# Expert stage of a fused audio tower: another order of its rows, a shorter bias product, and the fold ahead of the weight transposes

## What is computed

```
tok:   a = x W1 + b1;  8 times: up = relu(a + shift_r(up) W2 + b2), down likewise;  h = relu(c + ...)
attn:  h = h + (exp(-gamma * |q - k|^2) v) Wo^T          8 heads of 64, no softmax
ffn:   x = layernorm(h);  logits = x gate_w + gate_b;  top 2 of 16 experts, softmax over the two
       moe = sum over the two of weight * (relu(x w1[e] + b1[e]) w2[e] + b2[e])
       h = h + layernorm(x + moe) * gamma + beta
```

## Time and profile before

| | |
|---|---|
| median of three runs | 789.38 us (787.16, 789.38, 789.58) |
| profiled execution | 787.81 us, span of its instructions 785.9 us |
| busy, share of span | PE 95%, weight loads (PEld) 55%, DVE 80%, ACT 68%, POOL 59% |
| granted PE clock, mean | 0.991 |
| expert stage | about 505 to 783 us, steps of 16.5 us |

### The profile page before, as it was taken

One profiled execution on the slowest core, in us unless ns is written; L12 is line 12 of the kernel. 1 busy time (PEld: TensorE's weight loads), 2 busy tenths in 40 slices (PEclk: granted clock), 3 DMA queues, 4 the chain that ended last, 5 costly groups with the idle time before them and its releaser, 6 DMA issues.

```text
span 785.9 us, 16799 instructions
## 1 busy us (share of the span) xinstructions
PE 746.5 (95%) x5712; PEld 430.0 (55%) x5712; DVE 626.9 (80%) x1525; ACT 533.9 (68%) x1058; POOL 460.9 (59%) x625
## 2 busy tenths in 40 slices
PE   2999999999999999999999998999999999999992
PEld 1444356666666666676666665444555555454440
DVE  7676778888888888878888785788888888888862
ACT  1566779888888888888898887644555555546442
POOL 7644324544546454564545532267788787887877
PEclk9999999999999999999999999999999999999997
DMA  6300202211221112211122112000000000000000
GB/s 182 97 2 2 55 1 55 46 36 30 54 55 36 36 39 54 55 29 40 43 55 55 27 38 46 1 2 1 9 15 9 8 8 8 11 13 7 9 7 20
DMA packets 22619, 25.46 MB, mean 32 GB/s; under 512 B 12520, under 2 KB 21480, under 8 KB 22408
## 3 DMA queue, kind: packets, MB, share of 16 engines
q1 hardware_dynamic: 21544, 23.14, 12.6%
q10 hardware_dynamic: 992, 1.26, 0.7%
HBM read 5.06 MB, written 2.43 MB: 10 GB/s over the span
## 4 chain that ended last, share of the span: by engine, by line
PE 72%; DVE 13%; issue 6%; ACT 6%; POOL 2%; DMA 1%; ACTq 1%; POOLq 0%; SPq 0%; DVEq 0%
PE bank L1325 14%; PE bank L1303 14%; PE bank L1204 10%; PE bank L1162 9%; PE bank L1228 6%; PE bank L1075 5%; DVE m L819 5%; DVE prob L865 4%; PE bank L1230 4%; PE bank L1065 2%; ACT prob L601 1%; ACT m1o L560 1%; ACT m1e L560 1%; PE bank L1350 1%; PE bank L1342 1%
## 5 line engine op out<-in xcount | busy, mean ns | idle before, releaser
L429 POOL TENSOR_TENSOR sq<-sq 125x256 f32<-125x256 f32 x128 | 97.4, 772 | 162.3 <-ACT sq L565 137.7
L865 DVE TENSOR_SCALAR prob<-prob,cap_hi,cap_lo 125x500 f32<-125x500 f32 x256 | 156.1, 637 | 43.9 <-ACT prob L601 41.9
L601 ACT ACTIVATE prob<-bank 125x500 f32<-125x500 f32 x256 | 148.4, 591 | 39.0 <-PE bank L1230 37.1
L1303 PE MATMUL bank<-cs,w_sb 64*64 64x500 f32 x1024 | 147.1, 580 | 2.5 <-DVE gated L983 2.4
L1325 PE MATMUL bank<-gated,w_sb 64*64 64x500 f32 x1024 | 148.8, 588 | 0.0
L466 POOL TENSOR_TENSOR gated<-relu,wb 128x500 f32<-128x500 f32 x96 | 120.0, 1251 | 48.4 <-ACT relu L682 45.8
L983 DVE SCALAR_TENSOR_TENSOR gated<-bank,nb,wb 128x500 f32<-128x500 f32 x160 | 114.8, 727 | 34.6 <-PE bank L1303 34.6
L682 ACT ACTIVATE relu<-bank,b_sb 128x500 f32<-128x500 f32 x96 | 64.6, 673 | 92.7 <-PE bank L1303 92.7
L1303 PEld LDWEIGHTS bank<-cs,w_sb 64*64 64x64 f32 x1024 | 53.1, 133 | 55.1 <-issue 48.5
L1162 PE MATMUL bank<-wqku_hi,s 128*125 128x512 f32 x192 | 78.8, 410 | 0.5 <-DVE s L800 0.5
L565 ACT ACTIVATE sq<-bank 125x512 f32<-125x512 f32 x128 | 75.2, 599 | 4.7 <-PE bank L1162 1.0
(11 more groups left out here) (182 smaller groups left out, 1572.6 us busy)
## 6 DMA issues: line engine op xcount, KB each, us to landing
m1e<-m1e SPq DMA_DIRECT2D x64, 125.0 KB, 2.3
m1o<-m1o SPq DMA_DIRECT2D x64, 125.0 KB, 2.3
out<-res SPq DMA_DIRECT2D x16, 125.0 KB
w_sb<-in_w SPq DMA_DIRECT2D x1, 1024.0 KB
xa<-xparts SPq DMA_DIRECT2D x3, 281.2 KB
w_sb<-in_w SPq DMA_DIRECT2D x1, 512.0 KB
xw<-xparts SPq DMA_DIRECT2D x3, 140.6 KB
xparts<-x_part SPq DMA_DIRECT2D x3, 125.0 KB
```

The source lines that it names most:

```text
L429: gp.tensor_tensor(sq2[q][:, :, :], sq[q][:, :, 0:D // 2], sq[q][:, :, D // 2:D], ALU.add)\
L601: act.activation(prob[v % PROBS][:, :, c, :], bank[5 + n % 3][0:T, 0:C].rearrange("p (h l) -> p h l", h=2), ACT.Exp).then_inc(b_exp, 1)
L865: dve.tensor_scalar(part, part, cap_hi[0:T, h:h + 1], cap_lo[0:T, h:h + 1], ALU.min, ALU.max)\
L1303: last = pe.matmul(up_bank(g)[cols, 0:C], w1_sb[rows, g, cols], cs1[q % 3][rows, :], start=True, stop=True)
```

## The change

A row of an expert tile becomes copy * 16 + expert: `wtok` is written as [copy, expert], and w1, b1, w2 and b2 are laid out the same way on the host, with unchanged shapes. Each 64-row half of `wb` then holds the same four copies of the 16 weights.

Once, ahead of the first token transposes of the stage, PE multiplies `b2f` with a new constant that sums the 8 copies of an expert (128 more columns in `cst`), and ACT copies the result to `b2s`, whose halves each hold the 16 summed biases in their first rows and zeros below. `extra` uses one half for all: quarter tile c takes the tokens of chunk c, 125 instead of 250. PE waits for `b_gl` (all of attention's low parts) ahead of the sum and, in the first pair's `extra`, for the copy (`c_bias`); ACT waits for the product (`c_bsum`).

In slot 6 the fold of pair p - 2 stands ahead of the weight transposes of pair p.

```diff
--- before.py
+++ after.py
@@ -46,7 +46,8 @@
 C_W1, C_W2, C_MS1, C_MS2 = 128, 129, 130, 131
 C_IND = 132
 C_II = C_IND + H
-C_COLS = C_II + D
+C_SUM = C_II + D
+C_COLS = C_SUM + 128
 
 
 def constants():
@@ -64,6 +65,8 @@
     c[Q_ROW + H:Q_ROW + 2 * H, C_MS2] = -1.0
     c[K_ROW + H:K_ROW + 2 * H, C_MS2] = -1.0
     c[:, C_II:C_II + D] = np.tile(np.eye(D), (2, 1))
+    for half in (0, HALF):
+        c[:, C_SUM + half:C_SUM + half + E] = np.tile(np.eye(E), (R, 1))
     for h in range(H):
         c[K_ROW + h, C_IND + h] = 1.0
         c[K_ROW + H + h, C_IND + h] = 1.0
@@ -94,6 +97,7 @@
         b1_sb, nb1 = sb("b1_sb", [128, G]), sb("nb1", [128, G])
         w1_sb, w2_sb = sb("w1_sb", [128, G, 128]), sb("w2_sb", [128, G, D])
         b2raw, b2f = sb("b2raw", [128, D]), sb("b2f", [128, D])
+        b2s = sb("b2s", [128, D])
         fg_sb, fb_sb = sb("fg_sb", [T, D]), sb("fb_sb", [T, D])
 
 
@@ -123,7 +127,7 @@
         lg = sb("lg", [T, 8, CH, E])
         top = sb("top", [T, 12, CH])
         desc = sb("desc", [T, E])
-        wtok = sb("wtok", [T, CH, E, R])
+        wtok = sb("wtok", [T, CH, R, E])
         cagg, cvar = sb("cagg", [T, 2, CH, 2]), sb("cvar", [T, 2, CH])
         cneg, cinv, cnb = sb("cneg", [T, 2, CH]), sb("cinv", [T, 2, CH]), sb("cnb", [T, 2, CH])
         eps2, mhalf2 = sb("eps2", [T, 2, CH]), sb("mhalf2", [T, 2, CH])
@@ -168,6 +172,7 @@
         s_prep = sem("s_prep")
         s_prepg = sem("s_prepg")
         s_wprod = sem("s_wprod")
+        c_bsum, c_bias = sem("c_bsum"), sem("c_bias")
         a_xin, a_split, a_scr, a_table = sem("a_xin"), sem("a_split"), sem("a_scr"), sem("a_table")
         a_ones = sem("a_ones")
         a_xa = [sem(f"a_xa{i}") for i in range(ROUNDS)]
@@ -626,6 +631,8 @@
 
                 if v == 0:
                     normed(0)
+                    act.wait_ge(c_bsum, 1)
+                    act.activation(b2s[:, :], bank[4][:, 0:D], ACT.Copy).then_inc(c_bias, 1)
                     tokens_c(0)
                 else:
                     slot_c(0, v - 1)
@@ -972,7 +979,7 @@
                     done(dve.tensor_tensor(lg[:, 6, :, :], lg[:, 4, :, :], wide(top[:, 10, :]), ALU.mult))
                 if n == 17:
                     wait(dve, c_wt, p)
-                    first, second = (lg[:, k, :, :].unsqueeze(3).to_broadcast([T, CH, E, R]) for k in (5, 6))
+                    first, second = (lg[:, k, :, :].unsqueeze(2).to_broadcast([T, CH, R, E]) for k in (5, 6))
                     done(dve.tensor_tensor(wtok[:, :, :, :], first, second, ALU.add))
 
             def fused(q, g):
@@ -1277,6 +1284,9 @@
 
                 if v == 0:
                     pe.wait_ge(b_ev, 16 * PAIRS)
+                    pe.wait_ge(b_gl, 4 * PAIRS)
+                    pe.matmul(bank[4][:, 0:D], c_sb[:, C_SUM:C_SUM + 128], b2f[:, :], start=True, stop=True)\
+                        .then_inc(c_bsum, 1)
                     tokens_c(0)
                 else:
                     slot_c(0, v - 1)
@@ -1307,10 +1317,12 @@
             def extra(q):
 
                 pe.wait_ge(c_wbs, q + 1)
-                for cols, part in ((LO, slice(0, L)), (HI, slice(L, C))):
-                    for rows, y in ((LO, bank[0]), (HI, bank[1])):
-                        pe.matmul(y[cols, part], b2f[rows, :], wb[q % 2][rows, part], start=False, stop=False,
-                                  skip_group_check=True)
+                if q == 0:
+                    pe.wait_ge(c_bias, 1)
+                for c, (cols, rows, y) in enumerate(((LO, LO, bank[0]), (HI, LO, bank[0]), (LO, HI, bank[1]), (HI, HI, bank[1]))):
+                    part = slice(c * T, (c + 1) * T)
+                    pe.matmul(y[cols, part], b2s[rows, :], wb[q % 2][rows, part], start=False, stop=False,
+                              skip_group_check=True)
 
             def down(q, v):
 
@@ -1348,7 +1360,7 @@
                 wait(pe, c_wbs, p)
                 for c in range(CH):
                     last = pe.transpose(bank[3][:, c * T:(c + 1) * T],
-                                        wtok[:, c, :, :].rearrange("p e r -> p (e r)"), ident[0:T, 0:T])
+                                        wtok[:, c, :, :].rearrange("p r e -> p (r e)"), ident[0:T, 0:T])
                 last.then_inc(c_wt, 1)
 
             def fold_c(q):
@@ -1369,10 +1381,10 @@
                     if valid(p + 1):
                         tokens_c(p + 1)
                 if v == 6:
+                    if valid(p - 2):
+                        fold_c(p - 2)
                     if valid(p):
                         weights_c(p)
-                    if valid(p - 2):
-                        fold_c(p - 2)
                 if v < 3 and valid(p - 2):
                     down(p - 2, v + 5)
                 if v >= 3 and valid(p - 1):
@@ -1428,7 +1440,7 @@
     w_q, w_k, w_v = a("L0_attn_W_q"), a("L0_attn_W_k"), a("L0_attn_W_v")
     qT, kT, vT = (w.transpose(2, 0, 1) for w in (w_q, w_k, w_v))
     oT = a("L0_attn_W_o").reshape(D, H, D).transpose(2, 1, 0)
-    w1 = a("L0_ffn_w1").reshape(E, D, G, R)
+    w1 = a("L0_ffn_w1").reshape(E, D, G, R).transpose(1, 2, 3, 0).reshape(D, G, 128)
     arrays = {
         "cst": constants(),
         "xin": np.stack([x, x[:, ::-1]], axis=1),
@@ -1445,10 +1457,10 @@
         "lns": rows(a("L0_attn_ln_scale"), T),
         "gw": a("L0_ffn_gate_w"),
         "gb": rows(a("L0_ffn_gate_b"), T),
-        "w1": np.tile(w1.transpose(1, 2, 0, 3).reshape(D, G, 128), (2, 1, 1)),
-        "b1": a("L0_ffn_b1").reshape(E, G, R).transpose(0, 2, 1).reshape(128, G),
-        "w2": a("L0_ffn_w2").reshape(E, G, R, D).transpose(0, 2, 1, 3).reshape(128, G, D),
-        "b2": np.repeat(a("L0_ffn_b2"), R, axis=0),
+        "w1": np.tile(w1, (2, 1, 1)),
+        "b1": a("L0_ffn_b1").reshape(E, G, R).transpose(2, 0, 1).reshape(128, G),
+        "w2": a("L0_ffn_w2").reshape(E, G, R, D).transpose(2, 0, 1, 3).reshape(128, G, D),
+        "b2": np.tile(a("L0_ffn_b2"), (R, 1)),
         "fg": rows(a("L0_ffn_gamma"), T),
         "fb": rows(a("L0_ffn_beta"), T),
     }
```

## The result

The change makes the kernel slower. The median of four runs is 795.07 us (793.48 to 796.63) against 789.48 us before; the ratio is 1.0078 with an interval of 1.0049 to 1.0106. The forecast was 787.2 us in a range of 784.9 to 789.4. The profiled execution after took 793.48 us with a span of 791.6 us, 5.7 us more than the span before, at the same mean granted clock of 0.991. In what follows one execution, the first of experiment 1, ran with a mean granted clock of 0.752, took 940.36 us and is left out.

What follows compares the result with a forecast made beforehand. PE was taken to set the expert stage's 16.53 us step. Terms of -2.9 (bias product), +0.7 (fold order) and +0.1 (constants), -2.2 us with unrounded figures, gave 787.2 us, range 784.9 to 789.4.

Steps and rivals of the forecast that it cites:

- The step that failed: Expert stage: PE is busy for the whole 16.53 us step, so its saving shortens the step, to 16.37 us.
- Slower: DVE blocked behind POOL: Gate chain in a step's first half: DVE and POOL exclude each other, 1.0 us a step, total +11; 8% including milder.
- DVE takes over: Seventh up group: PE waits for DVE's `gated`, 0.2 us of room, saving lost, about 789.5 to 790 us; 10%.
- the bias product: `extra` (L1312): 125 columns instead of 250 save 0.21 us each, 14 times, 2.9 us; low end 0.14 each.
- The sum: Whole kernel: -2.9 + 0.7 + 0.1, with unrounded terms -2.2 us, so 787.2 us.
- the first fold load: Fold ahead of weight transposes: longer exposed load, about 0.05 us in 14 steps, +0.7 us, 0 as other bound.
- order of rows: `wtok` in the new order: 0 us, since slack covers even 0.6 us slower.
- summed bias and constants: Once: sum and copy 0, at worst 0.3 us; 128 more constant columns to load 0.1 us, at most 0.36.
- the stall behind the first bias product: PE's 1.29 us wait for DVE's `gated`: longer by 0.2 us, so no saving there.
- the one near the end: PE's 1.08 us stall in the step at 732: longer by 0.2 us, so no saving there.
- The slow clock goes: PE from 485.10 to 488.50: keeps the 2.4 GHz level instead of 1.2, -1.0 us, so 786.2 us; 13%.

Runs made afterwards that it cites:

- experiment 1: The kernel before with only the bias product cut to 125 columns on each quarter: 793.6 us, ratio 1.0062.
- experiment 2: The changed kernel with the bias product back at 250 columns, multiplying `b2f` in its old loop: 789.31 us, ratio 1.0004.
- experiment 3: The changed kernel with the weight transposes ahead of the fold again: 794.66 us, ratio 1.0071.
- Experiment 4: The changed kernel with POOL's gating of group 9 waiting for DVE's second gate product: 785.92 us, ratio 0.9961; repeated 786.05 us, 0.9969.
- 5: The kernel before with its bias product on 226, then 190 columns per quarter instead of 250: 787.8 us and 795.75 us.
- experiment 8: The changed kernel with both gate products moved behind DVE's gating of group 8, no wait on POOL: 786.72 us, ratio 0.9975.

## Why the prediction was wrong

The step that failed is the one that turns PE's saving into a shorter step: "PE sets the pace there, and what leaves its queue leaves the step, unless another engine is close behind". The other engine was close behind, and the shorter product itself made it slower: DVE's second gate product went from 0.21 to 1.28 us and DVE set a step of 17.03 us. The prediction had the mechanism as a rival, "Slower: DVE blocked behind POOL", at 8%, and a milder sister, "DVE takes over", at 10%, but gave it the wrong place, price and threshold.

*Place.* The prediction put the blocking in the first half of the step and set the half with the bias product aside: "those move together; the 0.2 us falls between `extra` and the end of the step". That is where it happened. The long L971 of the earlier trace rows stood there already, at 612.67, 12.9 us into the step and behind the bias product (611.25). The pair on POOL, `y_moe` and the gating of group 9, has its first member released ahead of the bias product and its second behind it, so just these two shift against each other. None of the prediction's rows is of POOL. There the 1.33 us between the two starts stood to be seen, where the pairs beside it (611.30 to 612.51, 617.19 to 618.40) follow each other in 1.21; only the pair behind it, 613.84 to 615.16 with DVE's `wtok` between, is 1.32 apart too.

*Threshold.* The prediction has it decide at a shift of some 0.5 us. In the kernel before it decides between 0.04 and 0.10 us, and the change shifts by 0.21.

*Price.* The rival took 1.0 us in 13 steps and took the saving off. DVE's instruction grew by 1.07 us, near enough. But a step pays only what exceeds DVE's slack. The chain at 17.02 us with L979 at 0.21 would be 17.02 - 1.07 = 15.95 us long. So, as an estimate from the trace after, DVE was 0.58 us from setting the step of 16.53; of the 1.07 us, 0.49 shows. The total was +5.6 us, not the rival's +11.

*Room.* "DVE takes over" counts 0.2 us of room for the seventh up group and a cost of at most 0.7 us. That room took the length of DVE's row as given. A length set by what POOL does was the one thing that couldn't be given.

*The sum.* With DVE kept out of the way most of its terms come out as forecast, which experiments 2, 3 and 4 show one by one:
- the bias product saved 0.21 us. Experiment 4 has the forecast step, 16.37 us, and a ratio of 0.9961 and 0.9969, where 0.9972 was forecast;
- the first fold load costs 0.05 us a step (16.53 to 16.58 in experiment 2, 17.03 to 16.98 in experiment 3). Idle time ahead of it is the same 0.79 us with no releaser, and from there to the next down product it is 1.06 us (618.71 to 619.77) as said. The first loads last 187 and 141 ns as before. The Trainium skill (TensorE: Matmul & The Clock Gate, LDWEIGHTS) has a load cost its columns and not its rows; these runs differ from it here too, 187 ns for 125 columns and 141 for 128, and the measurement decides. That the 128 rows are the reason isn't shown: in the trace before, loads of 112 rows by 125 columns (L1230) have a median of 187 ns as well;
- order of rows: `wtok` unhindered takes 0.68 us, before 0.67, and hindered 1.09 in experiment 2 as in the kernel before. 0, as said;
- summed bias and constants: nothing in experiment 2, where 0 and 0.1 us were forecast. The sum (L1288) runs at 482.15, ahead of 1.65 us of idle time of PE, its copy takes 0.20 us at 484.08, as PE's token transposes start (484.23), and the run's first recurrence matmul starts at 16.11 us, not later than before (16.65) for the larger constants;
- the stall behind the first bias product went from 1.29 to 1.50 us, by the 0.21 saved, as said; the one near the end from 1.08 to 1.14, less than said.

*The slow clock goes* did not come about. Busy times of the stretches before the stage and in it, of the kernel after:

```profile
481.00:484.40 3.40, 1.75 (x13) 0.86 (x12) 1.43 (x4) 2.18 (x7) 0.00 (x0) 0.99 0.14 31
484.40:487.80 3.40, 3.40 (x14) 2.83 (x15) 0.19 (x1) 1.76 (x3) 0.00 (x0) 0.51 0.00 0
```

PE was busy for 1.75 us ahead of it instead of 1.30, and then had the 1.2 GHz level (granted 0.51) for the same 3.4 us as in the earlier trace rows. In the profiled execution of experiment 2 it was 3.4 us too, in those of all other experiments about 6.8 us, whether they ran slower or faster than the kernel before. What decides between the two lengths is open. As an estimate, 3.4 us more at half the clock cost at most 1.7 us of a run, over half of what experiment 4 gains; the length of a steady step, at granted 1.00, is free of it, and the argument rests on that length.

The Trainium skill (SBUF — State Buffer, Who interferes with whom), which the prediction drew on, has DVE and GpSimd exclude each other for whole instructions. The rows agree: after, L978 ends 0.08 us behind the POOL product that it met (615.80 against 615.72) and L979 0.09 us behind its own (617.01 against 616.92). What fell short was the prediction's use of it: what the lock costs hangs on who is next in line, and that turned on less than a tenth of a microsecond.

What is shown: that the short product alone brings the loss (1, 2), that it goes with POOL's gap (4, 5), and that the stall is gone when the gating that PE waits for stands ahead of the held instruction (8, with L978 shorter as well). What is inferred from starts and durations alone is that the gap matters by letting DVE take its turn; no record shows the turn itself.

## What to carry to other kernels

When a change takes time off one engine, list for every other engine which of its instructions are released ahead of that place and which behind it: these shift against each other, and where DVE and POOL products meet, a shift of 0.1 us can turn an instruction of 0.2 us into one of 1.3. Look at the start-to-start times of POOL's products: where one stands a little wider than the rest and a DVE product lies in the gap, that gap may be what lets it through. A wait that keeps the gap open costs POOL some idle time (0.39 us here) and can protect the engine that sets the pace. Before pricing a longer instruction, work out how far its engine is from setting the step; only the rest is paid, and once it is paid, savings on the other engine pay next to nothing.

## What the hardware showed that I had not expected

- Where two POOL products follow each other directly, one held DVE product got in between and the next did not. L978 ended 0.08 us after `y_moe`; L979, right behind it on DVE, was held for POOL's whole next product and took 1.28 to 1.30 us for 0.21 us of work, in every steady step. In experiment 8 too the first of the pair came through (0.32 us) and the second was held.
- The gap that lets the second one in is small: POOL starts 1.28 us apart suffice and 1.22 don't, and DVE's start was then only 0.04 us ahead of POOL's. Each of the two figures is from one run.
- DVE's gating with its input in a PSUM bank and `wb` in SBUF took 701 to 740 ns in all its 160 places after, many beside POOL's products (616.93 beside POOL's at 616.90). A TENSOR_REDUCE of one SBUF input didn't stretch either (0.22 us at 613.44, beside POOL's product of 613.25). Those that stretched by more than 0.05 us, in the steady steps after, are TENSOR_TENSOR operations with both inputs in SBUF.
